# The depthwise product's two column tiles: two groups of channels, or the two halves of the image

## The reference

```
h = einsum('oc,bchw->bohw', w1, x)              # 48 -> 288 channels ("expand")
h = relu(bn(h, g1, b1, m1, v1))
h = depthwise 3x3 convolution(h, wd), 288 groups, padding 1
h = relu(bn(h, gd, bd, md, vd))
h = einsum('oc,bchw->bohw', w2, h)              # 288 -> 48 channels ("project")
return x + bn(h, g2, b2, m2, v2)
```

## Time and profile before

| | us |
|---|---|
| median of 3 runs | 1954.3 (1952.6 to 1955.3) |
| span of the profiled execution | 1952.0 |
| attention and perceptron, until the convolution's first chunk | about 1073 |
| first expand, without a chunk before it | 14 |
| one chunk (from depth 1 to the next depth 1) | 35.9 |

### The profile page before, as it was taken

How to read it: one execution, slowest core, us unless ns; L and a number is a source line. 1 busy time by engine, 2 the same in 40 slices (tenths; PEclk the granted TensorE clock), 3 DMA queues, 4 the chain that set the end, 5 groups by cost and what they waited for, 6 DMA issues and landing times.

```text
span 1952.0 us, 74705 instructions
## 1 busy us (share of the span) xinstructions
PE 1870.2 (96%) x29960; PEld 1565.2 (80%) x29960; DVE 1445.8 (74%) x2650; ACT 1322.8 (68%) x2838; POOL 647.1 (33%) x869
## 2 busy tenths in 40 slices
PE   5999999999999996999999999999999999999998
PEld 4888888888888885555555899999999999999997
DVE  5999999999999997666667556566566566566564
ACT  2788878878888885555555666666666666666665
POOL 4333333333333333413100434325334343344240
PEclk9999999999999998999999999999999999999999
DMA  2222222222222222777664444545363454445331
GB/s 67 68 73 76 78 73 76 77 73 76 77 72 77 74 76 77 182 171 179 161 150 111 97 108 126 99 113 126 87 147 86 112 137 102 103 129 105 99 111 34
DMA packets 286410, 198.43 MB, mean 102 GB/s; under 512 B 225991, under 2 KB 275672, under 8 KB 276504
## 3 DMA queue, kind: packets, MB, share of 16 engines
q1 hardware_dynamic: 282114, 189.12, 37.9%
q0 software_dynamic: 2368, 6.25, 1.5%
q10 hardware_dynamic: 1750, 0.39, 0.1%
HBM read 128.36 MB, written 54.72 MB: 94 GB/s over the span
## 4 chain that ended last, share of the span: by engine, by line
PE 56%; ACT 2%; DMA 1%; issue 1%; DVE 0%; SPq 0%; ACTq 0%; DVEq 0%
PE psum L1126 14%; PE psum L1145 13%; PE psum L1171 9%; PE psum L1180 5%; PE psum L680 5%; PE psum L661 3%; PE psum L651 3%; PE psum L666 2%; ACT h2T L1227 1%; DMA room<-tok_mid 1%; ACT h L884 1%; DMA room<-in_ident 0%; ACT room L750 0%; DVE room L885 0%; DVE room L712 0%
## 5 line engine op out<-in xcount | busy, mean ns | idle before, releaser
L934 POOL TENSOR_TENSOR mats<-mats,dscale 112x2048 f32<-112x2048 f32 x72 | 260.8, 3622 | 315.0 <-DMA mats<-in_taps 312.6
L1126 PE MATMUL psum<-ew,xp 64*100 64x96 f32 x6144 | 322.4, 252 | 16.8 <-ACT h L884 13.5
L885 DVE TENSOR_SCALAR h<-psum 100x384 f32<-100x384 f32 x384 | 211.9, 557 | 151.7 <-PE psum L1126 141.6
L1126 PEld LDWEIGHTS psum<-ew,xp 64*100 64x100 f32 x6144 | 295.5, 165 | 26.3 <-ACT h L884 18.6
L1227 ACT ACTIVATE h2T<-psum 96x1024 f32<-96x1024 f32 x192 | 195.6, 1019 | 177.5 <-PE psum L1180 177.5
L1145 PE MATMUL psum<-h,mats 101*64 101x128 f32 x4608 | 269.2, 274 | 1.6 <-issue 0.9
L1145 PEld LDWEIGHTS psum<-h,mats 101*64 101x64 f32 x4608 | 252.0, 137 | 11.8 <-issue 2.0
L884 ACT ACTIVATE room<-psum 64x512 f32<-64x512 f32 (+1 forms) x384 | 206.1, 537 | 78.1 <-PE psum L1145 71.5
L344 PE MATMUL psum<-kb,qa 128*64 128x256 f32 x2048 | 244.0, 380 | 0.8 <-DVE prob L443 0.8
L885 DVE TENSOR_SCALAR room<-psum 64x512 f32<-64x512 f32 (+1 forms) x288 | 174.2, 605 | 64.7 <-PE psum L1145 58.8
L884 ACT ACTIVATE h<-psum 100x384 f32<-100x384 f32 x384 | 186.6, 486 | 48.1 <-PE psum L1126 34.1
(11 more groups left out here) (154 smaller groups left out, 3228.3 us busy)
## 6 DMA issues: line engine op xcount, KB each, us to landing
mats<-in_taps SPq DMA_DIRECT2D x69, 896.0 KB, 5.9
tok_mid<-mid SPq DMA_DIRECT2D x128, 224.0 KB, 1.9
room<-tok_mid SPq DMA_DIRECT2D x64, 448.0 KB, 4.4
piece<-img_mid SPq DMA_DIRECT2D x196, 63.8 KB, 2.4
img_mid<-room SPq DMA_DIRECT2D x128, 97.5 KB, 3.0
kb<-kk SPq DMA_DIRECT2D x512, 24.0 KB
out<-yc SPq DMA_DIRECT2D x32, 384.0 KB, 4.5
scratch<-in_x_tokens SPq DMA_DIRECT2D x126, 96.0 KB, 1.9
```

The costliest lines, as they stand in the source:

```text
L885: return nc.vector.tensor_scalar(dst, src, 0.0, None, ALU.max)
L934: nc.gpsimd.tensor_tensor(m, m, bc(scale[0:MROWS, at:at + TCH], 2, POUT), ALU.mult).then_inc(mats_scaled, 1)
L1126: mm = nc.tensor.matmul(ring[(j + u) % 4][0:PIN, p:4 * CH:4], xp[hx][rows, 2 * j + p, :], w1[rows, c, :], start=True, stop=True)
```

## The change

Both column tiles now work on the same channel: tile r takes the patches of half r, 64 of them, and writes partitions 64r on. So a PSUM bank holds the left half image in its lower and the right one in its upper partitions, as h2 has it. A matmul streams 64 columns, not 128, and there are twice as many. A bank holds eight channels of both halves and is taken out by one instruction of 128 partitions. The depths use two banks each: depths 0 and 2 banks 0 and 1, 1 and 3 banks 2 and 3, depth 4 banks 4 and 5, depth 5 banks 6 and 7. The waits follow from that.

```diff
-        PARTS = [1] * (DEPTHS - 1) + [2]
-        READY = [sum(2 * n for n in PARTS[:d]) for d in range(DEPTHS + 1)]
-        ACT_OUT = [2 * sum(PARTS[:d]) + (2 if d else 0) for d in range(DEPTHS + 1)]
-        DVE_OUT = [2 * sum(PARTS[1:d]) for d in range(DEPTHS + 1)]
+        READY = [2 * d for d in range(DEPTHS + 1)]
+        ACT_OUT = [d + (1 if d else 0) for d in range(DEPTHS + 1)]
+        DVE_OUT = [max(d - 1, 0) for d in range(DEPTHS + 1)]
+        BANK_OF = (0, 2, 0, 2, 4, 6)
...
-        def evacuate_depthwise(by_act, d, u, part, r):
+        def evacuate_depthwise(by_act, d, part):
 
-            ch, bank, banks = DUNIT * d + DUNIT // 2 * u + 4 * part, 4 * (d % 2) + u + 2 * part, 2 // PARTS[d]
-            half = slice(2 * PATCHES * r, 2 * PATCHES * (r + 1))
-            dst = h2[POUT * r:POUT * r + POUT, :, ch:ch + 4 * banks].rearrange("q p (b n) -> q p b n", n=4)
-            src = psum[POUT * u:POUT * u + POUT, bank:bank + 2 * banks - 1:2, half].rearrange("q b (p n) -> q p b n", n=4)
+            ch = DUNIT * d + DUNIT // 2 * part
+            dst = h2[:, :, ch:ch + DUNIT // 2].rearrange("q p (b n) -> q p b n", n=4)
+            src = psum[:, BANK_OF[d] + part, :].rearrange("q (b p n) -> q p b n", b=2, n=4)
             return relu(by_act, dst, src)
...
                 elif not isinstance(k, int) or k > 0:
-                    pe.wait_ge(*((unit_dve, dve_before_expand(k) - 4) if j % 2 else (unit_act, act_before_expand(k) - 4)))
+                    pe.wait_ge(unit_act, act_before_expand(k) - 2)
+                    pe.wait_ge(unit_dve, dve_before_expand(k) - 2)
...
                 if d == 0:
                     emptied(k, 0)
-                if d >= 2:
+                elif d in (2, 3):
                     emptied(k, d - 1)
-                for n in range(DUNIT // 2):
-                    if d == 1 and n == 4:
-                        pe.wait_ge(y_done, NSTEP * k + 1)
-                    for u in range(2):
-                        ch = DUNIT * d + DUNIT // 2 * u + n
-                        bank = psum[POUT * u:POUT * u + POUT, 4 * (d % 2) + u + 2 * (n // 4), :]
-                        mm = nc.tensor.matmul(bank[:, n % 4:4 * PATCHES:4], mats[ch // TCH][0:PIN + 1, ch % TCH, :],
-                                              h1[0:PIN + 1, ch, :],
+                elif d == 4:
+                    pe.wait_ge(copied, NSTEP * k)
+                    pe.wait_ge(y_done, NSTEP * k + 1)
+                for n in range(DUNIT):
+                    ch = DUNIT * d + n
+                    at = 4 * (PATCHES // 2) * (n % 8 // 4) + n % 4
+                    for r in range(2):
+                        mm = nc.tensor.matmul(psum[POUT * r:POUT * r + POUT, BANK_OF[d] + n // 8, at:at + 4 * (PATCHES // 2) - n % 4:4],
+                                              mats[ch // TCH][0:PIN + 1, ch % TCH, :],
+                                              h1[0:PIN + 1, ch, PATCHES // 2 * r:PATCHES // 2 * (r + 1)],
                                               start=True, stop=True)
-                        if (n + 1) % (DUNIT // 2 // PARTS[d]) == 0:
-                            mm.then_inc(unit_ready, 1)
+                    if n % 8 == 7:
+                        mm.then_inc(unit_ready, 1)
```

More of the change, by code:

```diff
@@ L1213, in filtered @@
                 for d in range(DEPTHS):
[L1214 to L1218, removed]
+                    for part in range(1 if d else 2):
+                        act.wait_ge(unit_ready, ready_before_depthwise(k) + READY[d] + part + 1)
+                        evacuate_depthwise(True, d, part).then_inc(unit_act, 1)
             def chunk(b, hx, c, last):
@@ L1245, in filtered @@
                 for d in range(1, DEPTHS):
[L1246 to L1249, removed]
+                    dve.wait_ge(unit_ready, ready_before_depthwise(k) + READY[d] + 2)
+                    evacuate_depthwise(False, d, 1).then_inc(unit_dve, 1)
             def add(n, b, hx, c, k):
```

## The result

The changed kernel takes 1987.1 us (median of 4, 1984.2 to 1988.0) against 1953.9 of the kernel before: ratio 1.017, 95% interval 1.0155 to 1.0184. It is slower by 33 us. 1973 was forecast, within 1947 to 1990.

A forecast was written before the change was run, and what follows sets the result against it. The prediction took TensorE's stream of records to bound the kernel. From a span of 1952.0 us it took 3.0 for parts 1 to 3, added 22 for fetches (1971.0), then 2.3 from span to median: 1973 us, range 1947 to 1990.

The forecast's parts named there:

- Matmuls: Depthwise product: 384 records a chunk at 29.1 ns instead of 192 at 54.8, +0.65 us a chunk.
- The line from 26 to 96 streamed columns (37 ns): Upper estimate of depthwise record spacing at 64 streamed columns, drawn between two other matmul lines: 37 ns, where 29.1 was taken.
- Evacuation: One 128-partition instruction replaces two of 64 after depthwise matmuls: -0.57 us a chunk, -1.0 once in chunk 0, -0.7 once at the end.
- The ring's wait: TensorE's idle for a free one of four banks, at the third expand unit after the depthwise product: 0.75 us to 0.18.
- Banks and waits: Depthwise product's new bank assignment moves the wait for VectorE's add from depth 1 to depth 4: -0.16 us a chunk.
- The wait for yc: TensorE's depth 1 idle for VectorE's last add into yc, expected to vanish: 0.16 us a chunk.
- parts 1 to 3: Matmuls, Evacuation, Banks and waits together: -0.08 us in a usual chunk, -3.0 us in all.
- its wait of 1.82 us: TensorE's idle ahead of the last chunk's transposes, expected to shrink to about 1.1 us, -0.7 once.
- Fetches: Depthwise product: instruction fetches need 3.0 to 7.1 us but get 3.7 plus 0.5, beside mats reloads: +1.0 us a chunk, +22.
- hidden fetches: Rival: instruction fetches in the depthwise product cost nothing, leaving parts 1 to 3 alone: 1951 us, chance 0.28.
- A slower array: Rival: depthwise records take 33 ns instead of 29, +2.15 us a chunk, fetches mostly hidden: 1987 us, chance 0.10.
- The ring not freed: Rival: evacuation engines stay late for expand's banks, 13 us more than each case, 1964 with hidden fetches; chance 0.06.

The follow-up runs named there:

- reverse experiment: Changed kernel with each reload of mats cut to one partition, and each depthwise evacuation cut into two of 64 partitions: 1961.8 us, against 1947.4 without the evacuation cut.
- half reloads: Changed kernel with each reload of mats cut to 56 of 112 partitions (448 KB): 1958.3 us, ratio 1.0019 to the kernel before.
- the records alone: Kernel before with each depthwise matmul issued as two of 64 columns; banks, waits and evacuations unchanged: 1990.7 us, ratio 1.0180.

## Why the prediction was right, and where its sizes were off

The direction, the mechanism and the range held. The forecast of 1973 was 14 us too low. Two errors lie behind that and partly cancel: fetches cost 17 us more than the 22 of the sum, and the rest of the change gained some 4 us more than the 3.0 of the sum. By its steps:

1. *Matmuls.* 29.1 ns a record was forecast and is measured. The line from 26 to 96 streamed columns (37 ns) was no bound that mattered. Depths 1 to 5 of an undisturbed chunk take 9.4 us. In the paragraph on what bounds the kernel I gave all six instructions on ScalarE (2.81 us) to the last depth; two of them are depth 4's, as part 2 reckons. In the sum for the last chunk I wrote that 320 records become 640; it is 160 that become 320, and the +0.54 us was worked out from the right ones.

2. *Evacuation.* The ring's wait was to fall from 0.75 to 0.18 us and is 4.5 / 22 = 0.20 without reloads. The reverse experiment gives 14.4 us against 14, of which one late fetch is 1.4.

3. *Banks and waits.* The wait for yc is gone, 0.16 us a chunk, and no new one took its place. What I had left out: before, TensorE also stood some 0.05 to 0.1 us at the edges of depths 3 and 5, where VectorE's two instructions of 0.69 us left only 0.3 us of room in 1.75; they are gone too. I take it that the banks did that and not the one instruction, for in the run with each evacuation cut in two depths 1 to 5 are as long as without the cut, 9.28 us from the first start to the last. (A depth of the kernel before waits until the depth two before it is taken out, not the one before, as I wrote of `emptied`; the prediction has it right.) A quiet chunk is 786.7 / 22 = 35.76 us against 35.93, -0.17 instead of the -0.08 of the sum. So parts 1 to 3 were sized at -3.0 us in all, and without reloads the change gives 1947.4 - 1954.2 = -6.8. The two profiled runs place it: 4.1 us in the 22 chunks (1.8 in the sum), 1.1 in chunk 0 (0.9), 1.8 in the last (0.3). In the last there is something that I didn't see: behind its wait of 1.82 us the kernel before runs 3.4 us at half clock (so it does without reloads), and the changed one, with 0.99 us of wait, doesn't. The window of before:

```profile
1931.70:1935.10 3.40, 3.32 (x36) 2.84 (x38) 0.75 (x1) 1.22 (x3) 0.00 (x0) 0.50 0.00 0
```

4. *Fetches.* Named as what decides, with place, cause and mark in the profile, and that is what came: one stall a chunk, at block ends, behind the reloads. The size was the mis-sized term: +22 us forecast, 39 measured over 22 chunks. The step that failed is "I take 0.5 on the mean, nearer the lower end, since the whole convolution of before shows just these two stalls". That two stalls were all said little: at 6 to 7 us a block nearly every delayed fetch was still in time, and at 3.7 us the same delays show. One stall of 1.3 us a chunk came (27.9 / 21, without the two at L1182), where the sum has two of 0.5; the middle of 0 to 2.9 us for one fetch a chunk would have been 1.45, which is easily said afterwards. A second part was not in the sum at all: the half clock behind the stalls, 6 us in these chunks. Two terms of the step had no row: the 0.6 us until a packet starts and the 0.5 by which the sequencer runs ahead. The traces show them only together: without reloads a packet of q8 starts 0.45 us (median) after TensorE has begun the block before (a block counted from the place of the stalls), and 0.6 us ahead of that at the earliest. And of the two stalls of before I wrote that expand had both; the second lies ahead of a projection.

The Trainium skill (Runtime: NRT & Kernel Launch, instruction fetch mechanics) is borne out in its block of 256 instructions: 36 more packets for 9216 more records. That the fetch is hidden holds for the changed kernel only when no large load is queued ahead: 1947 us without the reloads and 1951.5 with them paced, against 1987.

The rivals: *hidden fetches* would have been 1951; the run without reloads shows what that world looks like, 1947. *A slower array* is refuted by 29.1 ns over 320 records without a break. *The ring not freed* is refuted by 0.20 us of wait where 0.75 was, and by the experiment on the evacuation alone.

## What to carry to other kernels

Before splitting matmuls into shorter ones, divide the fetch interval by the new pace: here one fetch per 256 instructions of TensorE, 7 us apart before and 3.7 after. With 896 KB loads queued ahead, the blocks that ended in a stall of over 0.5 us lasted 4.6 to 7.2 us with the stall, and that is about the time such a fetch needed. Idle of TensorE over 0.3 us whose only reason was "issue" and that came back at one place in a block of 256 instructions was that fetch. "Issue" alone is no proof of it: with the reloads later, 10.1 us of it stood at other places and came from a store. It was cheaper to cut the large loads into parts that wait for each other than to move them: that took 35.6 us back, while the same loads put later cost 8 us more, because pieces of the image and stores came to stand behind them.

## What the runs showed of the hardware that I had not expected

- From the landing of a late block to TensorE's next record 1.2 to 1.7 us passed, in all 24 stalls of the changed kernel.
- Behind a stall of 1.6 us, in a stretch in which TensorE had been busy without a break for 7 us, the granted clock fell to half for 3.4 us and 71 records took 3.7 us, 52 ns each. Four other stalls of the changed kernel did the same, 19 did not, the longest of 2.5 us among them; with stalls of 1.5 us at most (half reloads) no chunk did. What decides was not tested.
- Evacuations of 512 columns take the same time from 64 partitions as from 128: 590 and 597 ns on ScalarE, 694 and 692 on VectorE.
- Two costs on one engine don't add up if the first gives others time: in the run with the records alone, the ring's wait is 6.9 us instead of 16.5.
- Stores delay a fetch as loads do: with the reloads gone, one stall of 1.4 us was left in one run, behind two stores of 384 KB.
